# A two-layer transformer kernel on one core: attention scores from float32r parts in two row tiles instead of bf16 parts in four column tiles, and TensorE's order in slots

## The reference

```python
# A: grouped-query attention, 4 key/value heads
attn = softmax(einsum('bghnd,bhsd->bghns', q, k) * D_Q ** -0.5)   # 512 x 512 scores a head
# M: latent attention: layernorm'd latent of 64, rotary q and k, causal mask
scores = einsum('bhqd,bhkd->bhqk', q, k) / sqrt(HEAD_DIM)
scores = where(causal, scores, -inf)
# then a mixture of 4 experts, top 1, hidden 512 (relu), chosen by argmax(x @ gate_w.T + gate_b)
# B: attention with one key/value head; feed-forward of 384 with weights given as int32
```

## Time and profile before

| | |
|---|---|
| time, median of 3 runs | 2816.89 us (2811.06 to 2822.78) |
| profiled execution, span from first to last instruction | 2813.9 us |
| PE busy | 2628.6 us (93%) |
| DVE busy | 2305.2 us (82%) |
| ACT busy | 1727.4 us (61%) |
| POOL busy | 791.1 us (28%) |
| mean granted PE clock | 0.978 |

### The profile page before, as it was taken

One profiled execution on the slowest core, in us unless ns is written; L12 is line 12 of the kernel. 1 busy time (PEld: TensorE's weight loads), 2 busy tenths in 40 slices (PEclk: granted clock), 3 DMA queues, 4 the chain that ended last, 5 costly groups with the idle time before them and its releaser, 6 DMA issues. The chain is left out here.

```text
span 2813.9 us, 121706 instructions
## 1 busy us (share of the span) xinstructions
PE 2628.6 (93%) x51440; PEld 1437.3 (51%) x51440; DVE 2305.2 (82%) x6003; ACT 1727.4 (61%) x3522; POOL 791.1 (28%) x1369
## 2 busy tenths in 40 slices
PE   5969999999999999999999999999999999999958
PEld 2435454645546465464645546464554646546432
DVE  5758879798898979889797988979889897988825
ACT  1725756666576666757666575766657566675725
POOL 4132422223241222423223242222324122242110
PEclk7979999999999999999999999999999999999987
DMA  3041221403112041221304122140312214132120
GB/s 98 7 125 36 79 76 32 125 25 108 55 59 89 26 135 30 89 73 36 113 25 123 43 77 79 31 125 25 110 52 67 81 29 133 29 90 73 34 71 6
DMA packets 168048, 191.30 MB, mean 68 GB/s; under 512 B 24614, under 2 KB 150736, under 8 KB 167504
## 3 DMA queue, kind: packets, MB, share of 16 engines
q1 hardware_dynamic: 163408, 175.12, 20.4%
q0 software_dynamic: 4096, 8.40, 1.0%
HBM read 84.18 MB, written 16.25 MB: 36 GB/s over the span
## 5 line engine op out<-in xcount | busy, mean ns | idle before, releaser
L1208 ACT ACTIVATE probs<-bank 128x512 f32<-128x512 f32 x2688 | 1463.7, 599 | 678.2 <-PE bank L615 670.6
L966 DVE TENSOR_REDUCE mx<-bank 128x1 f32<-128x512 f32 x2048 | 1281.2, 682 | 62.4 <-PE bank L615 49.3
L971 DVE CUSTOM_DVE_ANT_0 bank<-bank,mask 128x128 f32<-128x128 f32 (+3 forms) x1024 | 478.5, 517 | 109.2 <-PE bank L615 101.7
L615 PE MATMUL bank<-kp_B,qp_B 72*32 72x512 bf16 x4096 | 439.9, 390 | 18.5 <-DVE mx L966 9.2
L615 PE MATMUL bank<-qp_B,kp_B 74*32 74x512 bf16 x4096 | 413.5, 382 | 3.1 <-ACT probs L1208 1.7
L615 PE MATMUL bank<-qp_A,kp_A 74*32 74x512 bf16 x4096 | 408.5, 380 | 6.8 <-DVE mx L966 6.2
L615 PE MATMUL bank<-kp_A,qp_A 72*32 72x512 bf16 x4096 | 394.8, 381 | 12.4 <-DVE mx L966 7.5
L615 PE MATMUL bank<-kp_M,qp_M 72*32 72x128 bf16 (+3 forms) x4096 | 318.4, 311 | 32.0 <-DMA kp_M<-parts_k 23.5
L1353 POOL TENSOR_SCALAR nms<-mx 128x16 bf16<-128x16 f32 x192 | 39.5, 206 | 1087.1 <-DVE mx L971 509.6
L615 PE MATMUL bank<-qp_M,kp_M 74*32 74x128 bf16 (+3 forms) x4096 | 297.5, 302 | 20.0 <-DVE mx L966 15.2
L736 PE MATMUL pv<-probs,vv_B 128*32 128x512 f32 x2048 | 274.8, 594 | 1.2 <-ACT probs L1208 1.0
(11 more groups left out here) (167 smaller groups left out, 3286.4 us busy)
## 6 DMA issues: line engine op xcount, KB each, us to landing
wxs<-wx SPq DMA_DIRECT2D x112, 578.0 KB, 4.1
qp_M<-parts_q SPq DMA_DIRECT2D x144, 128.0 KB
kp_M<-parts_k SPq DMA_DIRECT2D x144, 128.0 KB
qp_A<-parts_q SPq DMA_DIRECT2D x144, 128.0 KB
qp_B<-parts_q SPq DMA_DIRECT2D x144, 128.0 KB
xp<-xq SPq DMA_DIRECT2D x16, 448.0 KB, 7.3
kp_A<-parts_k SPq DMA_DIRECT2D x144, 32.0 KB
xs<-x SPq DMA_DIRECT2D x16, 256.0 KB, 3.0
```

Source lines behind the costliest of these rows:

```text
L615: ins = pe.matmul(dst[at:at + n], lhsT[:, at:at + n], rhs, start=start, stop=stop, tile_position=(0, at))
L966: v.tensor_reduce(mx[:, g % 2, at:at + 1], s1[BANK[a, g, u]][:], AX.X, ALU.max) \
L971: v.tensor_tensor_reduce(bank[:, 0:keys], bank[:, 0:keys], mask[:, SEQ - keys:SEQ], 1.0, LOWEST, ALU.add, ALU.max, mx[:, g % 2, at:at + 1] ...
L1208: act.activation(probs[:, slot, :], s2[BANK2[a, g, u]][:], ACT.Exp).then_inc(sig[f"{a}_exp"], 1)
```

## The change

- `split` makes two float32r parts (rounded copy, remainder) instead of three bf16 ones: two POOL operations instead of four. `pack` issues four DMAs instead of nine, of float32 width.
- Queries and keys of two neighbouring heads share a block of 512 columns: the even head lies in partitions 0 to 63, the odd one in 64 to 127. In each half row 8c + r holds part r // 2 (queries) or r % 2 (keys) of channel c, rows 62 and 63 hold the maximum, and the rest is zero. The zeros are written once at the start, by ACT (M), DVE (queries of A) and POOL (the others).
- A first score is one matmul of 60 rows by 128 columns instead of four of 72 by 32. `score_exp` does two units (an even and an odd head) at once, with 64 rows by 128 columns each. M's mask is two matmuls of 64 columns for each part, in the same half of the rows.
- `score_max` and `score_exp` have the same time for both units of a pair. PE's order, and with it the order of the banks, is sorted into eighths of a unit (`in_slots`): in each slot the first scores stand first, then the second scores, then everything else. The other engines keep their orders. `lag` goes from 1.986 to 2.0.
- The float32 matmuls (probabilities by values, projections, feed-forward) keep their column tiles of 32.

```diff
+SLOTS = 8
...
-                put(s + g + u / 16, "score_max", a, g, u)
+                put(s + g + u // 2 / 8, "score_max", a, g, u)
...
-                put(s + T["lag"] + g + (u + 0.5) / n, "score_exp", a, g, u)
+                put(s + T["lag"] + g + u // 2 * 2 / n, "score_exp", a, g, u)
...
+def in_slots(rows):
+
+    kinds = {"score_max": 0, "score_exp": 1}
+    return sorted(rows, key=lambda row: (int(SLOTS * row[0] + 1e-6), kinds.get(row[2], 2), row))
...
-    table = ordered()
+    table = in_slots(ordered(LATE["PE"]))
...
-            return qp[a][0:rows, h, :]
+            return qp[a][HALF * (h % 2):HALF * (h % 2) + rows, h // 2, :]
...
-            return kp[a][0:rows, KHEAD[a](h), :]
+            return kp[a][HALF * (h % 2):HALF * (h % 2) + rows, KHEAD[a](h), :]
...
-                in_columns(s1[BANK[a, g, u]][:, 0:keys], q_rows(a, h, ROWS1)[:, P * t:P * t + P],
-                           k_rows(a, h, ROWS1)[:, 0:keys]).then_inc(sig[f"{a}_s1_ps"], 1)
+                pe.matmul(s1[BANK[a, g, u]][:, 0:keys], q_rows(a, h, ROWS1)[:, P * t:P * t + P],
+                          k_rows(a, h, ROWS1)[:, 0:keys], start=True, stop=True).then_inc(sig[f"{a}_s1_ps"], 1)
...
+                pair = (u, u + 1)
+                for v in pair:
+                    for s_last, value in last_user(b, turn_bank, BANK2[a, g, v], f"{a}_exp", UNITS2[a] * g + v + 1):
+                        pe.wait_ge(s_last, value)
+                for both in zip(*(unit_parts(a, v) for v in pair)):
+                    ins = {}
+                    for v, (hh, c, col, q) in zip(pair, both):
+                        h = GROUP * g + hh
+                        ins[v] = pe.matmul(s2[BANK2[a, g, v]][:, col:col + q], k_rows(a, h, ROWS2)[:, P * c:P * c + P],
+                                           q_rows(a, h, ROWS2)[:, SEQ - q:SEQ], start=True, stop=a != "M")
                     if a == "M":
-                        ins = in_columns(scores[:, 0:P], identb[:], late_keys[:], False, True)
-                ins.then_inc(sig[f"{a}_s2_ps"], 1)
+                        for k in range(2):
+                            for v, (hh, c, col, q) in zip(pair, both):
+                                half = slice(HALF * (hh % 2), HALF * (hh % 2) + HALF)
+                                ins[v] = pe.matmul(s2[BANK2[a, g, v]][:, col + HALF * k:col + HALF * k + HALF],
+                                                   eye2[half, k, :], late_keys[half], start=False, stop=k == 1)
...
-                chain(b, f"{s}_split", 2, pool.tensor_tensor(r, f, p[0:n, 0, :], ALU.subtract))
-                chain(b, f"{s}_split", 3, pool.tensor_scalar(p[0:n, 1, :], r, 1.0, 0.0, ALU.mult, ALU.add))
-                chain(b, f"{s}_split", 4, pool.tensor_tensor(p[0:n, 2, :], r, p[0:n, 1, :], ALU.subtract))
+                pool.tensor_tensor(p[0:n, 1, :], f, p[0:n, 0, :].bitcast(F32), ALU.subtract).then_inc(sig[f"{s}_split"], 1)
```

More of the change, by code:

```diff
@@ L28 @@
 F32 = mybir.dt.float32
+F32R = mybir.dt.float32r
 BF16 = mybir.dt.bfloat16
@@ L577, in pack @@
                         sp.wait_ge(sig[f"{a}_s1_ps"], total(b.prev, f"{a}_s1_ps"))
-                    if b.first and s == "mq":
-                        sp.wait_ge(minus_set, 16 * 3)
+                    if b.first:
+                        sp.wait_ge({"mq": zero_act, "mk": zero_act, "aq": zero_dve}.get(s, zero_pool), 1)
+                    if b.first and not is_q:
+                        for n in range(2):
+                            sp.dma_start(kp[a][SHIFT + n:P:HALF].bitcast(F32),
+                                         minus[:].bitcast(F32).unsqueeze(1).broadcast_to([2, KBLOCKS[a], SEQ])) \
+                                .then_inc(minus_set[a], 16)
                 if is_q:
-                    dst, src = qp[a][r:ROWS1:PRODUCTS], parts["q"][:, r // PARTS, :]
+                    dst, src = qp[a][r:P:PITCH], parts["q"][:, r // PARTS, :]
                 else:
-                    dst, src = kp[a][r:ROWS1:PRODUCTS], parts["k"][0:KCH[a], r % PARTS, :]
-                sp.dma_start(dst, src).then_inc(sig[f"{s}_packed"], 16)
+                    dst, src = kp[a][r:P:PITCH], parts["k"][0:KCH[a], r % PARTS, :]
+                sp.dma_start(dst.bitcast(F32), src.bitcast(F32)).then_inc(sig[f"{s}_packed"], 16)
             def o_proj(b, a):
@@ L723, in probs_v @@
+                for v in pair:
+                    ins[v].then_inc(sig[f"{a}_s2_ps"], 1)
             def probs_v(b, a, g, r):
@@ L829, in _ @@
                          o_turn=o_turn, o_proj=o_proj, gate=gate, ranks=ranks, xp_turn=xp_turn, up=up, down=down, ff_up=ff_up, ff_down=ff_down)
[L830 removed]
+            walk(steps)
         @block.vector
@@ L1141, in _ @@
             act.activation(table_loaded[:], half_neg[:], ACT.Exp)
+            for side in (qp, kp):
+                ins = act.activation(side["M"][:].rearrange("p h n -> p (h n)"),
+                                     half_neg[:, 0:1].broadcast_to([P, PAIRS * SEQ]), ACT.Copy, scale=0.0)
+            ins.then_inc(zero_act, 1)
             act.wait_ge(ld_w, 16 * 5)
@@ L1289, in values_setup @@
                         link(pool.memset(vv[a][:, :, h, one:one + 1], 1.0))
+                link(pool.memset(eye2[:], 0.0))
+                link(pool.memset(late_keys[:], 0.0))
+                for at in (0, HALF):
+                    half = slice(at, at + HALF)
+                    for k in range(2):
+                        eye = eye2[half, k, HALF * k:HALF * k + HALF]
+                        link(pool.affine_select(out=eye, in_=eye, compare_op=ALU.not_equal, fill=1.0, base=0,
+                                                pattern=[[-1, HALF]], channel_multiplier=1))
+                    link(pool.affine_select(out=late_keys[half], in_=late_keys[half], compare_op=ALU.is_ge, fill=MASKED,
+                                            base=0, pattern=[[1, HALF]], channel_multiplier=-1))
+                    link(pool.memset(eye2[at:at + 1], 0.0))
+                    link(pool.memset(eye2[at:at + 1, 0, HALF:P], 1.0))
+                    link(pool.memset(late_keys[at:at + 1], MASKED))
                 pool.memset(seen[:], 0.0).then_inc(setup_pool, 1)
@@ L1336, in split @@
                 n = P if s[1] == "q" else KCH[s[0].upper()]
-                f, r, p = full[s[1]][0:n, :], rest[0:n, :], parts[s[1]]
+                f, p = full[s[1]][0:n, :], parts[s[1]]
                 pool.wait_ge(sig[f"{s}_full"], total(b, f"{s}_full"))
```

88 lines of the change are left out of this document (46 added, 42 removed).

## The result

The kernel after takes 3049.95 us (median of 4 runs, 3045.43 to 3060.73), the kernel before 2815.57 (4 runs beside them). The ratio is 1.084, with a 95% interval of 1.0814 to 1.0866: 234 us slower, where 2720 with 2600 to 2880 was forecast.

What follows compares the result with a forecast made beforehand. PE decides some stretches, but DVE is nearly at its limit in more than half of the period. Stretch terms -1.7, -1.6 and -3.0 make -6.3 us a batch, times 14 -88, edges -8: 2718, so 2720 us, range 2600 to 2880.

Steps and rivals of the forecast that it cites:

- the other three stretches: 97.7 us of a batch's period where DVE is nearly at its limit; DVE at 0.962 needs 94.7, so -3.0 us.
- PE's own fall: In those three stretches PE falls from 93.9 to 81 us: halved streaming -20.5, 65 tiling changes +7.8.
- slots bunch PE's other work: Objection to the full DVE gain: seven banks hold about a slot and a half of scores, so DVE still waits.
- Streaming saved: Score matmuls on PE: a pair of 512-column units takes 0.219 us instead of 0.438; -10.4 us in the stretch from 1167.2.
- Loads and mask: PE in the stretch from 1167.2: loads not hidden under M's narrow pairs +3.1 us, mask +1.2 us.
- Mode changes: PE switching between score tiles and 32-column tiles: 111 new changes a batch at 0.12 us, 13.3 us a batch.
- Edges: Start and last B: fewer split operations and DMAs save 5 us at each, setup gives back some 2; net -8 us.
- DVE everywhere: Rival: DVE bounds all stretches, -18 us a batch, 2555 us; with the half-way case, chance 0.21.
- half of that gain: Rival: half the gain of DVE bounding everywhere, 2640 us, as likely; chance 0.21 for the two together.
- Mode changes cost more: Rival: dearer tiling changes on PE; no gain at 0.26 us each, 2890 us at 0.35; slower by dearer changes, chance 0.10.
- float32r at two cycles: Rival: two cycles a column or no overlap, so no streaming saved; +11 us a batch, 2970 us; chance 0.08.
- The clock falls: Rival: PE's clock drops to 0.50 in DVE's stretches, +64 us a batch; a tenth of that time gives 2815; chance 0.03.

Runs made afterwards that it cites:

- e11: Kernel before (bf16 parts, column tiles) with pairs of maxima and pairs of exponentials at one time, lag 2.0, sorted by time without slots; 3008.11 us, ratio 1.0682.
- e1: Kernel before with only the changed kernel's order (pairs at one time, slots, banks by that order), bf16 parts and column tiles kept; 2973.45 us, ratio 1.0556.
- e6: Kernel before, order and bf16 parts kept, scores and mask in full-width tiles instead of four column tiles; 2995.31 us, ratio 1.0627.
- e8: Kernel after with six banks in turn instead of seven, nothing else changed; 3250.84 us, ratio 1.1534.
- e7: e1 (slots, pairs, bf16 parts) with scores and mask in full-width tiles instead of column tiles; 3076.15 us, ratio 1.0914.
- g1: Kernel after, with a pair's second exponential score waiting for its bank just before its own matmul; 3032.91 us, ratio 1.0784.
- f1: Kernel before with only the maxima at one time in pairs, exponentials single; 2887.30 us, ratio 1.0268.
- f3: Kernel before with single exponentials, all put 0.048 of a unit earlier; 2848.21 us, ratio 1.0129.
- f2: Kernel before with only the exponentials at one time in pairs, lag 2.0; 2912.91 us, ratio 1.0359.
- g2: Kernel before with all exponentials put 0.024 of a unit later; 2849.68 us, ratio 1.0132.
- e5: Kernel after's float32r parts and row tiles with the old times, old order and banks, and single exponentials; 3068.49 us, ratio 1.0887.
- e12: Kernel before with six banks in turn instead of seven; 2915.53 us, ratio 1.0354.

## Why the prediction was wrong

**The failed step** is the sum's treatment of "the other three stretches": "PE falls from 93.9 to 81. DVE at 0.962 needs 94.7 of the 97.7 there: -3.0". It took the best twelfth of before as what DVE reaches wherever PE needs less than DVE. In those three stretches DVE reached 0.857, 0.859 and 0.884 after the change, while PE was busy 0.856, 0.889 and 0.845 of them: neither decides, and each waits for the other, which the sum put at nothing. The share of 0.962 belonged to an order in which single units of the two kinds alternated. Put in pairs, with the same matmuls, they cost 192 us (e11), and 156 once sorted into slots (e1). The table has the same across all edits: of the time that a kernel lost, between 69 and 104% is found again as more waiting of DVE for PE (e1 153 of 156, e6 173 of 177, after 225 of 234, e8 405 of 432). DVE's work is the same in all of them, so a loss must show as DVE standing; what the column adds is that PE is named. Why PE is late it doesn't tell: in e6 PE is busy 2849 of 2994 us, and its own time decides there.

PE's own fall failed too. In the three stretches PE was busy 91.6 us, not 81, and from 1260 to 1320.5, where it was to fall to 52.4, 54.9. By the sum's own counts, 65 and 37 changes at 0.21 for 0.12 make 5.9 and 3.3 of this, and the lower clock from 1320.5 to 1350.8 up to 5 more. Over the run PE's busy time fell by 8 us, where 16.2 a batch were summed. The objection that "slots bunch PE's other work" and that "DVE still waits in crowded slots" stood in the text, but only against the case of a larger gain; it should have been a rival on the slower side.

**Streaming saved:** right in price. A pair of 512 columns is followed after 0.24 (0.219 taken), and PE's busy time shows 249 us saved against e7. What it buys was wrong: 26 us, or 43 if each unit waits for its own bank (g1).

**Loads and mask:** the loads as taken, the mask cheaper. Loads of 128 float32r columns run under the matmuls ahead of their own (1212.27, for the pair at 1212.50), and four mask matmuls, for which 0.22 was taken, are followed after 0.07 where scores come next (1293.75 to 1293.82) and after 0.18 ahead of the values, a change of tiling included (1294.62 to 1294.80).

**Mode changes:** right in kind, mis-sized. 0.12 was taken and 0.21 measured in after; between full-width bf16 tiles and column tiles it is 0.115, as taken. Put into the forecast's own formula, 0.21 gives -2.1 a batch and 2780: under its break-even of 0.26, and far from 3050. In e7 the same 111 changes cost 103 us (7.4 a batch; 13.3 expected). The drain at a change of tiling mode that the Trainium skill, TensorEngine Tiling (Array Packing), Key Properties, states agrees with the late starts between these tilings: 0.42 a round trip with 64-row tiles, 0.23 with full-width ones, and none where column tiles follow column tiles (1113.62 to 1114.70 above, 0.22 and 0.86).

**Edges:** predicted -8, not seen. Timeline of the start:

```profile
32.76 1.27 POOL L1385 TENSOR_TENSOR parts_k<-full_k,parts_k 128x512 fp32r<-128x512 f32 x1
...
34.06 1.29 SPq L593 DMA_DIRECT2D kp_M<-minus  x2
35.39 3.63 SPq L600 DMA_DIRECT2D kp_M<-parts_k  x4
```

The four packs take 3.63 where nine took 5.81 (under 3 expected), but two DMAs of `minus` stand 1.29 ahead of them, and the second load of x starts at 126.09, 9 us later than before (117.07). At the end, the last batch's output follows the one before it after 105.9 us instead of 113.6.

**The rivals.** "DVE everywhere" and "half of that gain" fell with the step above. "Mode changes cost more" has the right sign and about half of the loss (103 of 234 in the new order, 177 in the old one with 152 changes). float32r at two cycles fell by the 0.24. "The clock falls" came in part: 0.83 in one stretch of 30.3 us, 0.955 over the run against 0.978. At 0.83 PE had the lower level for about a third of that stretch, 10 us, which at the full level would be 5; 14 times that is at most 72 us. It isn't the whole: e6 loses 177 at a mean clock of 0.975. But it is a part in every run with pairs. In e1, 1285.7 to 1300.5, PE stands at DVE's banks (0.53, 0.29 and 0.95 us, the last until 1300.37), and the next stretch is at 0.65, with DVE short of work (timeline, then stretches with columns as in the earlier trace rows):

```profile
1300.37 0.57 PE L622 MATMUL bank<-kp_A,qp_A 72*32 72x512 bf16 x4 [0.95 <-DVE mx L973]
```

```profile
1285.74:1300.49 14.75, 12.44 (x276) 6.74 (x265) 14.40 (x37) 7.60 (x15) 3.65 (x7) 1.00 0.07 17
1300.49:1315.24 14.75, 14.72 (x177) 6.38 (x174) 9.80 (x16) 4.59 (x9) 5.19 (x7) 0.65 0.02 4
```

An estimate from the table's mean clocks: as the lower level is 0.50, twice what a mean lacks to 1.00 is the share of the span spent there, and half of what that time grows by is the most that the full level would give back. That is 82 us of e11's 192, 63 of e1's 156, 45 of f1's 75, 29 of f3's 36, 20 of f2's 101 and 18 of g2's 37.

**The path from before to after**, medians: pairs +192 (e11), slots -35 (e1), 111 changes of tiling +103 (e7), float32r in two row tiles -26. By this path the order takes two thirds of the 234 us. The parts don't add, though, and another path divides them otherwise: full-width tiles first +177 (e6, 184 changes a batch), then pairs and slots +81 (e7, 143 changes), then float32r -26. With float32r in the old order the kernel is 250 us slower (e5), more than with the new one. So the order costs 81 to 157 among bf16 units, the changes 103 to 177, and on either path the changes take more than the streaming gives.

**Open:** why units in pairs cost so much, and how much of it is the clock, which no run held. That the banks' lead is eaten is argued: with seven banks in turn, two of a kind come free together from one reader while the other reader has none; e8 and e12 show only that a bank is worth more in the new order (201 against 100 us). More banks weren't tried. Also open is why float32r singles in the old order (e5) are 73 us slower than full-width bf16 (e6); the dearer change of tiling, 0.21 for 0.115, would suffice (two first scores after values in e5 are followed after 0.35 as well, 1225.44 to 1225.79), but no run separates it. No version tried beats the kernel before.

## What to carry to other kernels

An engine's share in the best stretch belongs to the order that ran there. When an edit changes the order in which shared buffers go to two readers, cost the order by itself first: here it lost 156 us with the same matmuls, and could be run without the rest. Don't add up the parts of a change that meet in the same waits; run them in more than one sequence. Count the changes of tiling in the order (0.1 to 0.2 us each here) before taking a faster tile. And when a busy engine is relieved, look for who hands its buffers back: 249 us of saved streaming returned as 220 us of standing.

## What was new of the hardware

- A change between two 64-row float32r tiles and 32-column tiles delays PE by 0.21 us (half of a round trip's 0.42), between full-width bf16 and 32-column tiles by 0.115.
- Two float32r matmuls of 64 rows by 128 columns, in two row tiles, stream 512 columns each within 0.24 us together; one kept waiting for its bank takes its time alone (g1: a pair's two matmuls span 0.96). Without pairs, matmuls of the two row tiles start out of the table's order (e5).
- A shift of 0.024 to 0.048 of a unit in one kind's place (0.3 to 0.7 us of a 13.9 us unit) costs 1.3% here (in part by the clock), and one PSUM bank of seven 3.5 to 6.6%.
